# An audio tower on one core: ScalarE and VectorE instead of GpSimd split the weights of the 64-expert mixture

## What is computed

```python
# sparse attention: 8 heads of 16, u = 25 rows per head are attended
Q, K, V = x @ Wq, x @ Wk, x @ Wv            # x = layernorm(h)
QK_sample = einsum('bhld,bhsd->bhls', Q, K[:, :, idx_sample, :]) * scale
M = QK_sample.max(axis=-1) - QK_sample.mean(axis=-1)
_, top_idx = top_k(M, u)
attn = softmax(einsum('bhud,bhld->bhul', Q[top_idx], K) * scale)
out = V.mean(axis=2) for all rows, attn @ V for the rows of top_idx
h = h + out @ Wo
# mixture of 64 experts of 128 x 256, 42 of them for each token
hid = gelu(einsum('td,edh->teh', x, w1) + b1)     # x = layernorm(h)
y   = einsum('teh,ehd->ted', hid, w2) + b2
h   = h + einsum('ted,te->td', y, comb)
```

## Time and profile before

| | |
|---|---|
| median of 3 runs | 2250.52 us (2250.28 to 2256.35) |
| the profiled execution | 2254.79 us |
| its span in the trace | 2253.1 us |
| sampling stage (trace) | 543.3 to 669 us, choice to 681.7 |
| `attend` | 681.7 to 849.7 us |
| n4 | 849.7 to 876.6 us |
| second mixture | 876.6 to 2253 us |
| busy over the span | PE 85%, DVE 79%, POOL 64%, ACT 60% |
| mean granted clock of PE | 0.914 of full |

### The profile page before, as it was taken

The page is one execution under the profiler, slowest core; times in us unless marked ns, Lnnn a source line. Parts: engine busy times, 40 slices in busy tenths (PEclk is TensorE's granted clock), DMA queues, the critical chain, the costliest instruction groups (busy, mean ns, idle before and its releaser), DMA issues.

```text
span 2253.1 us, 35345 instructions
## 1 busy us (share of the span) xinstructions
PE 1920.4 (85%) x9464; PEld 1057.5 (47%) x9464; DVE 1785.7 (79%) x2821; ACT 1356.3 (60%) x2002; POOL 1444.3 (64%) x1090
## 2 busy tenths in 40 slices
PE   7999103678986886589999999999999999999998
PEld 5566102456655885334444444444444444444444
DVE  4874602753568774989999999999999999999998
ACT  3113202522432453578888878888878888888887
POOL 2100373007968305368888888888888888888887
PEclk9999656985996897589999999999999999999999
DMA  3512013402324103133444454444454444444443
GB/s 85 161 38 85 21 52 80 78 9 75 128 75 131 56 1 134 51 110 135 138 138 136 137 211 135 135 139 142 142 206 140 139 141 141 141 147 147 147 147 114
DMA packets 122751, 257.24 MB, mean 114 GB/s; under 512 B 40212, under 2 KB 56244, under 8 KB 121012
## 3 DMA queue, kind: packets, MB, share of 16 engines
q1 hardware_dynamic: 119988, 250.78, 35.0%
q0 software_dynamic: 2688, 5.44, 0.8%
HBM read 219.13 MB, written 29.59 MB: 110 GB/s over the span
## 4 chain that ended last, share of the span: by engine, by line
PE 51%; DVE 5%; issue 2%; DMA 1%; POOL 0%; ACT 0%; DVEq 0%; SPq 0%; ACTq 0%; POOLq 0%
PE bank L2172 27%; PE bank L2186 24%; DVE hc L2104 1%; DMA m_share<-expert_shares 1%; DVE hc L2108 1%; DVE bank L2101 1%; DVE m_work L2086 1%; PE bank L2193 0%; DVE m_best L2083 0%; DVE h L2112 0%; DVE m_work L2077 0%; DVE m_ut L792 0%; ACT bank L2024 0%; DVE m_best L2076 0%; PE bank L784 0%
## 5 line engine op out<-in xcount | busy, mean ns | idle before, releaser
L2024 ACT ACTIVATE bank<-bank,m_b 128x896 f32<-128x896 f32 x768 | 753.2, 981 | 197.0 <-PE bank L2172 196.4
L1981 POOL TENSOR_TENSOR hc<-hc 128x896 f16<-128x896 f32 x384 | 725.3, 1889 | 31.9
L2186 PE MATMUL bank<-hc,weights 128*128 128x448 f16 x3072 | 707.2, 353 | 8.3 <-DVE h L2112 7.0
L1979 POOL TENSOR_SCALAR hc<-hc 128x896 f16<-128x896 f32 x384 | 359.8, 937 | 167.9 <-PE bank L2186 129.3
L2104 DVE TENSOR_TENSOR hc<-bank,m_share 128x896 f32<-128x896 f32 x384 | 419.1, 1091 | 48.1 <-ACT bank L2024 4.7
L2172 PE MATMUL bank<-m_u_first,weights 128*128 (+1 forms) x1536 | 422.2, 357 | 24.1 <-DVE hc L2104 11.4
L2186 PEld LDWEIGHTS bank<-hc,weights 128*128 128x128 f16 x3072 | 298.3, 98 | 297.5 <-issue 15.3
L2101 DVE TENSOR_TENSOR bank<-bank,m_share 128x896 f32<-128x896 f32 x384 | 418.7, 1090 | 10.4 <-ACT bank L2024 6.2
L2108 DVE TENSOR_TENSOR hc<-bank,hc 128x896 f16<-128x896 f32 x384 | 415.4, 1082 | 5.4 <-ACT hc L2027 5.4
L2172 PE MATMUL bank<-m_u_second,weights 128*128 (+1 forms) x1536 | 418.1, 354 | 0.0
L2027 ACT ACTIVATE hc<-bank 128x896 f16<-128x896 f32 x384 | 352.0, 917 | 37.8 <-DVE bank L2101 25.7
(11 more groups left out here) (320 smaller groups left out, 2221.4 us busy)
## 6 DMA issues: line engine op xcount, KB each, us to landing
m_share<-expert_shares SPq DMA_DIRECT2D x384, 448.0 KB, 3.6
ew_raw<-e_w_dram SPq DMA_DIRECT2D x32, 512.0 KB, 4.5
expert_factors<-ew_made SPq DMA_DIRECT2D x24, 512.0 KB, 3.0
weights<-expert_factors SPq DMA_DIRECT2D x12, 1024.0 KB, 9.1
expert_slots<-lru_zeros SPq DMA_DIRECT2D x1, 7296.0 KB, 28.5
lru_wst<-w_dram SPq DMA_DIRECT2D x16, 256.0 KB, 2.7
weights<-w_dram SPq DMA_DIRECT2D x1, 4096.0 KB, 12.5
xs<-x_dram SPq DMA_DIRECT2D x4, 996.0 KB, 12.3
```

The lines of the kernel that those rows point to most:

```text
L1979: g.tensor_scalar(h_first[:, x, 1], hs[:, x], 1.0 - SHARE, 1.0, ALU.mult, ALU.mult).then_inc(first_of[1], 1)
L1981: g.tensor_tensor(h_second[:, x, 1], hs[:, x], h_first[:, x, 1], ALU.subtract).then_inc(second_of[1], 1)
L2024: sc.activation(bank, bank, ACT.Gelu, bias=b1[:, bass.ds(grp * GE + e, 1), c]).then_inc(gelu[c], 1)
L2186: last = t.matmul(banks_y[:, q], k.weights[:, grp % 2, 2 + m, at], hh[:, e % 2, c, q * HW:(q + 1) * HW], start=(grp > 0 and e == 0 and c = ...
```

## The change

POOL makes no more pieces. ACT makes the rounded factor (`act_first`) and the raw piece times 64 (`act_wide`, into a new two-slot tile `wide`); DVE makes the second factor from both in one operation (`dve_second`). In the sampling stage chunk c takes piece c: ACT rounds it after the copies of quarter 1 and widens it after those of quarter 3; DVE finishes piece c - 1 after the measure of quarter 1, and piece 15 after the chunks. In `attend` piece 16 + b / 2 is rounded in the even step b and widened in the odd one after it; DVE finishes the piece before at the end of the even step. n3 and n4 make none. Loads are issued two ahead of the stores. The loops of ACT and DVE in both stages are written out; POOL's diagonals go into a hardware loop. The uses of `norm_statistics` lose their argument `pieces`, and the sync and POOL parts that it ran.

```diff
@@ -1186,11 +1177,9 @@
                        allow_small_or_imprecise_dtypes=True).then_inc(made, 1)
-                first, end = PIECES_SAMPLE
-                for c in range(NC):
-                    norm.pool_diagonal(pool, c, c % 2)
-                    if 1 <= c <= end - first:
-                        k.expert_weights.pool_pieces(pool, first + c - 1, first + c)
+                with pool.Fori(0, NC // 2) as i:
+                    for j in range(2):
+                        norm.pool_diagonal(pool, 2 * i + j, j)
                 g.memset(expand[:], 0.0).then_inc(made, 1)
@@ -1217,8 +1206,12 @@
                         last.then_inc(kx_copied, 1)
-
-                chunks(act, work)
+                        if q == 1:
+                            k.expert_weights.act_first(act, c)
+                    k.expert_weights.act_wide(act, c)
+
+                for c in range(NC):
+                    work(c, c % 2)
                 act.wait_ge(step_pe, 1)
@@ -1260,6 +1253,8 @@
                                         sc[:, :, NS:NS + 1].rearrange("p a b -> p (a b)"), ALU.subtract).then_inc(measured, 1)
+                        if q == 1 and c:
+                            k.expert_weights.dve_second(dve, c - 1)
 
@@ -1276,7 +1271,9 @@
                 link(v.memset(cand[:], SENT))
-                chunks(dve, work)
+                for c in range(NC):
+                    work(c, c % 2)
+                k.expert_weights.dve_second(dve, NC - 1)
 
@@ -1441,15 +1438,6 @@
 
-        def batches(eng, step):
-
-
-            for x in range(U):
-                step(x, x)
-            with eng.Fori(1, B // U) as i:
-                for x in range(U):
-                    step(U * i + x, x)
-
         def exists(b):
@@ -1472,8 +1460,6 @@
                                 pattern=[[NU, NH], [0, DH]], channel_multiplier=-1).then_inc(made, 1)
-            k.expert_weights.pool_pieces(pool, *PIECES_ATTEND)
-
         @block.scalar
@@ -1513,8 +1499,13 @@
                 output_copy(b - 2, x - 2)
-
-            batches(act, step)
+                if b % 2 == 0:
+                    k.expert_weights.act_first(act, NC + b // 2)
+                else:
+                    k.expert_weights.act_wide(act, NC + b // 2)
+
+            for b in range(B):
+                step(b, b)
             exponentials(B - 1, B - 1)
@@ -1598,9 +1589,10 @@
                 residual(b - 3, x - 3)
-
-            batches(dve, step)
-            for b in range(B, B + 3):
+                if b % 2 == 0 and 2 <= b <= B:
+                    k.expert_weights.dve_second(dve, NC + b // 2 - 1)
+
+            for b in range(B + 3):
                 step(b, b)
@@ -1721,7 +1713,7 @@
 GROUP = 2 * PIECES
-PIECES_N3, PIECES_SAMPLE, PIECES_ATTEND, PIECES_N4 = (0, 5), (5, 19), (19, 29), (29, NG * GROUP)
+PIECES_SAMPLE, PIECES_ATTEND = (0, NC), (NC, NG * GROUP)
 
@@ -1736,11 +1728,10 @@
         self.raw = sb("raw", [128, 2, PIECE])
-        self.left = sb("left", [128, PIECE])
+        self.wide = sb("wide", [128, 2, PIECE])
         self.made = sb("made", [128, 2, 2, PIECE], F16)
...
         self.rounded = k.semaphore("ew_rounded")
-        self.raw_read = k.semaphore("ew_raw_read")
         self.widened = k.semaphore("ew_widened")
@@ -1755,7 +1746,7 @@
         if n >= 2:
-            sp.wait_ge(self.raw_read, n - 1)
+            sp.wait_ge(self.widened, n - 1)
         first = n // GROUP * GE * HC * 128 + n % PIECES * PIECE
@@ -1767,33 +1758,35 @@
     def sync_pieces(self, sp, first, end):
-        self.sync_load(sp, first)
+        for n in range(first, min(first + 2, end)):
+            self.sync_load(sp, n)
         for n in range(first, end):
-            if n + 1 < end:
-                self.sync_load(sp, n + 1)
+            if n + 2 < end:
+                self.sync_load(sp, n + 2)
             self.sync_keep(sp, n)
...
 
-    def pool_pieces(self, pool, first, end):
-        g = self.nc.gpsimd
-        for n in range(first, end):
-            raw, left, out = self.raw[:, n % 2, :], self.left[:], self.place(n)
-            pool.wait_ge(self.raw_in[n % 2], 16 * (n // 2 + 1))
-            if n - 2 >= GROUP:
-                pool.wait_ge(self.k.kept_out[n % 2], 16 * ((n - GROUP) // 2))
-            g.tensor_copy(out[:, 0], raw).then_inc(self.rounded, 1)
-            pool.wait_ge(self.rounded, n + 1)
-            if n:
-                pool.wait_ge(self.split, n)
-            g.tensor_tensor(left, raw, out[:, 0], ALU.subtract).then_inc(self.raw_read, 1)
-            pool.wait_ge(self.raw_read, n + 1)
-            g.tensor_scalar(left, left, 1.0 / SHARE, 1.0, ALU.mult, ALU.mult).then_inc(self.widened, 1)
-            pool.wait_ge(self.widened, n + 1)
-            g.tensor_tensor(out[:, 1], left, out[:, 0], ALU.add).then_inc(self.split, 1)
-
-
+    def act_first(self, act, n):
+        act.wait_ge(self.raw_in[n % 2], 16 * (n // 2 + 1))
+        if n - 2 >= GROUP:
+            act.wait_ge(self.k.kept_out[n % 2], 16 * ((n - GROUP) // 2))
+        self.nc.scalar.activation(self.place(n)[:, 0], self.raw[:, n % 2, :], ACT.Copy).then_inc(self.rounded, 1)
+
+    def act_wide(self, act, n):
+        if n >= 2:
+            act.wait_ge(self.split, n - 1)
+        self.nc.scalar.activation(self.wide[:, n % 2], self.raw[:, n % 2, :], ACT.Copy, scale=1.0 / SHARE).then_inc(self.widened, 1)
+
+    def dve_second(self, dve, n):
+
+
+        out = self.place(n)
+        dve.wait_ge(self.rounded, n + 1)
+        dve.wait_ge(self.widened, n + 1)
+        self.nc.vector.scalar_tensor_tensor(out[:, 1], out[:, 0], 1.0 - 1.0 / SHARE, self.wide[:, n % 2], ALU.mult,
+                                            ALU.add).then_inc(self.split, 1)
 
@@ -2269,13 +2262,13 @@
             nc.all_engine_barrier()
-        norm_statistics(nc, k, "n2", 4, None, CW, TW, NCW)
+        norm_statistics(nc, k, "n2", 4, CW, TW, NCW)
         first_mixture(nc, k)
...
             k.expert_weights = ExpertWeights(nc, k, inner)
-            norm_statistics(nc, k, "n3", 5, PIECES_N3)
+            norm_statistics(nc, k, "n3", 5)
             sparse_attention(nc, k)
-            norm_statistics(nc, k, "n4", 6, PIECES_N4, CW, TW, NCW)
+            norm_statistics(nc, k, "n4", 6, CW, TW, NCW)
         second_mixture(nc, k, out)
```

More of the change, by code:

```diff
@@ L364, with norm_statistics @@
 DEEP, AHEAD = 4, 3
-def norm_statistics(nc, k, name, table, pieces=None, width=CH, tile=HALF, count=NC):
+def norm_statistics(nc, k, name, table, width=CH, tile=HALF, count=NC):
     tiles = count * (width // tile)
@@ L381, in norm_statistics @@
         v = k.bank[0:tile, DEEP, 0:tiles]
-        if pieces:
-            @block.sync
-            def _(sp):
-                k.expert_weights.sync_pieces(sp, *pieces)
-            @block.gpsimd
-            def _(pool):
-                k.expert_weights.pool_pieces(pool, *pieces)
         def span(c):
```

## The result

The changed kernel takes 2276.1 us (median of 5 runs, 2271.3 to 2281.5) where the kernel before takes 2252.2 beside it: a ratio of 1.0104, 95% interval 1.0081 to 1.0128. It is slower by 24 us; forecast were 33, and the time lies in the range. The profiled execution took 2281.5 us and is the longest of the five.

What follows compares the result with a forecast made beforehand. PE was taken to bound sampling, DVE and its chain `attend`. Terms +27.6 + 15 + 0.5 + 1.2 - 5.6 - 5.9 = +32.8 on a median of 2250.5 gave 2283.3 us, range 2262 to 2296.

Steps and rivals of the forecast that it cites:

- The wait for the store: Sampling: rounding pieces 10 to 15 waits for the store of the piece two before; 4.6 us in six chunks, +27.6.
- the faster rival: Sampling: second factor and store come early enough that no rounding waits; -9.8, 2240.7 us; chance 0.12.
- ACT can't pass the waiting operation: Sampling: ACT's queue is strictly first in, first out, so copies wait behind the rounding; otherwise the 27.6 would be 0.
- The clock: Sampling: PE's pauses in six chunks bring its clock to half speed, 2.5 us each, +15.
- The ends of sampling: Sampling: first rounding delays two quarters' copies, +0.5; last second factors delay measures and the candidates' copy, +1.2.
- `attend`: Stage `attend`: without POOL's pieces, steps of 4.55 and 4.91 us, -4.7; one-hots of step 0 freed, -0.9; together -5.6.
- n4: Stage n4: its end no longer waits for last piece and store, -5.0; a scalar operation freed, -0.9; together -5.9.
- n3 at 0: Stage n3: its pieces were hidden and its end is PE's, so removing them was costed at 0.

Runs made afterwards that it cites:

- the first cure: The changed kernel, but in the sampling stage DVE finishes piece c, not c - 1, after the measure of quarter 1 of chunk c; 2241.3 us, ratio 0.9941.
- the filled pause: The changed kernel with six unread products on PE ahead of the second sampled keys of chunks 10 to 15; 2267.1 us, ratio 1.0058.

## Why the prediction was right, and where it wasn't

*The wait for the store: right, in size too.* Forecast were six waits, a pause of PE of 4.45 us each and +27.6 us. The trace has six waits and pauses of 4.1 to 4.5; with the clock held up, the stage is 27.9 us longer than before. Two runs show the cause by taking it away in two ways, the store earlier and a third slot; a third leaves the wait and moves it in the queue. That this wait would not be there, the faster rival, is refuted.

*ACT can't pass the waiting operation: right.* The copies of quarters 2 and 3 wait with it (ACT idle 4.92 us ahead of L1775, then the rounding, six copies and the widening without a gap), as the Trainium skill says of its queue, "TensorE: Matmul & The Clock Gate", section "Architectural detail: the array is 16× 32×32, not 1× 128×128". The run with the rounding last shows that a wait for that store need not cost its length: 10.9 us of waits in six, 3.9 us in the stage.

*The clock: right in kind, too large in size.* Forecast +15, measured 11.9. I took 2.5 us for each of six pauses, from 5.3 us of work at half speed; the half-speed work after them was 6.4 us at first and 3.4 in the fourth and fifth, and they cost 3.1 down to 1.7, the sixth 0.8. I had the clock down in the middle of the pause, and it fell near its end or just after it. That waits between bursts bring the clock down and that it is paid in every turn, as the Trainium skill has it in "TensorE: Matmul & The Clock Gate", section "HAM oscillation — how this bites in real kernels", the trace bears out; that every burst starts slow it does not, since the fourth and fifth began at full clock and slowed within a microsecond.

*The ends of sampling, +1.7.* The sampling stage has no such surplus over the kernel before: 121.2 us in the first cure for 121.4. The loops written out give 1.2 us there (120.2), which I had not counted; over that, the work on ACT and DVE costs the first cure 1.0.

*`attend`: the step of the forecast that failed is its step time.* Forecast were 4.55 us for a step bound by ACT and 4.91 for one bound by DVE, 9.46 for the pair, and -5.6 in all; the stage is 10.5 us shorter. The maxima after:

```profile
752.64 0.49 DVE L1556 TENSOR_REDUCE att_nmax<-bank 100x2 f32<-100x332 f32 x1
...
756.62 0.50 DVE L1556 TENSOR_REDUCE att_nmax<-bank 100x2 f32<-100x332 f32 x1 [0.29 <-PE bank L1628]
...
761.80 0.49 DVE L1556 TENSOR_REDUCE att_nmax<-bank 100x2 f32<-100x332 f32 x1
```

The steps take 3.98 and 5.18 us in turn, 9.16 for the pair: one as short as a bare step, and one longer by the whole second factor, 1.2 us. So neither step is what I had forecast, and the two misses cancel but for 0.3 us; that the pair came near is in part luck. I worked with the rows of a looped kernel for a kernel without these loops; two bare steps are 0.2 us shorter without them, which is most of that 0.3. ACT's copies alone make each step 4.42 us (forecast 4.55), which was right, but with DVE's part beside them it isn't ACT's step that the trace shows.

*n4: -4.1 instead of -5.9.* The hold by POOL's last piece is gone, and the operation that took 0.91 us takes 0.18. But after the change n4 began at a clock of 0.60 in its first 4 us, and before at 1.00; where it began at 1.00 again, in the run with five pieces in n3, it took 28.4 us, 6.0 less than before. The second trace of the changed kernel has 0.50 in the first 4 us and 32.5 us for the stage. So the term was right, and the clock took 1.8 us of it back, or 4.0. What brought the clock down there isn't shown: PE's pauses at the end of `attend` are within 0.2 us of those before.

*n3 at 0: open.* Its length follows the clock. With POOL's pieces in it, the run with five pieces in n3 took 61.6 us for that part; without them, three variants took 61.2 to 61.6 too, but the changed kernel took 46.5 in both its traces. The last section has what speaks for a part of the change in that.

The sum: 27.9 + 11.9 for 27.6 + 15 + 1.7, and -0.5 - 10.5 - 4.1 for -11.5. The slow side was forecast 4.5 us too large, the clock above all, and the fast side 3.6 too small, `attend` above all; so the time came out 7 us under the forecast.

## What to carry to other kernels

Before an operation with a wait is put into the queue of an engine that feeds the bounding one, ask what is queued behind it and at which point of the loop the thing waited for is made, and not only whether the engine has time left: here both engines had it, and it cost 40 us. The cure is as small as the fault: one slot more, or the producer one turn earlier. And on PE a pause can be dearer than its length (here 27.9 us of waiting cost another 11.9), so a wait should be priced with the clock that it loses.

## What the runs showed of the hardware that I had not expected

The part from the first mixture's last `m_hsum` product to the first query, with n3 in it, takes either 60.7 to 61.8 us or 44.9 to 46.7. In the first case the granted clock stays at 0.50 through all of n3 though PE is busy without a gap over most of it. In the second it is back at 1.00 over the same work, in the changed kernel's trace from the window of 531 to 535 us on. The changed kernel was in the second in both its traces, other variants with the same n3 in the first:

```profile
520.00:548.00 28.00, 23.57 (x107) 18.24 (x106) 7.62 (x18) 4.09 (x9) 21.49 (x16) 0.50 0.16 42
```

```profile
520.00:548.00 28.00, 24.02 (x164) 17.96 (x162) 11.04 (x25) 9.42 (x19) 0.32 (x2) 0.80 0.00 1
```

The first is the kernel before, the second the changed one: in the same time 164 products for 107. Of the five traces with pieces on POOL in n3 none had the short form, of the seven without four had it. The lists of times point the same way. Of 78 executions of kernels with pieces in n3 (54 of the kernel before, 24 of its variants) none lies more than 5.6 us under the median of its list. Without pieces in n3 such executions are common: with the rounding last three of ten lie at 2230 to 2234 and six at 2245 to 2251, one each of the first cure, of the three slots, of the filled pause and of the changed kernel's second list lies 11 to 17 us under its median, and without second factors in `attend` three of four lie at 2224 and one at 2236. So taking POOL's pieces out of n3 seems to be what makes the short form possible, which the forecast had at 0. That is argued from lists and not shown: I have no run that changes n3 alone, and what decides between the two forms in one and the same kernel is open. The 14 us are as large as what many changes are worth, so single executions are to be compared by stage and not by their sum.
